# Fewer semaphore signals in three edge passes: counting steps in pairs, and the logit and state chains woven together

## The chip, the cores and the metric

One core of one Trainium2 chip runs the whole program. The metric is device time in microseconds of that core, as the median over runs.

## The reference

The reference is a graph network of 6250 nodes with 96 features and 200,000 edges sorted by destination, run as four blocks, each with a residual and a layer norm. What the change touches is the per-edge work of the first two blocks:

```python
# block 0, attention (4 heads): e = leaky_relu(a_src[src] + a_dst[dst], 0.2)
m = segment_max(e, dst); e = exp(e - m[dst]); denom = segment_sum(e, dst)
out = segment_sum((e / denom[dst])[:, :, None] * h[src], dst)
# block 1, twice: msg = x[src] @ W_msg + edge_attr @ W_edge
agg = segment_max(msg, dst)                   # 0 where a node has no edge
# blocks 2 and 3: sums over the edges of a node, five times (mean, mean, GCN x3)
```

## The kernel before, in words

The edges lie in order over 128 partitions, 1568 edges to a partition. An edge pass works through them in 196 slots (`SLOTS`) of 8 edges a partition (`S`). There are three such passes: the attention pass, and two maximum passes (`MAX_PASSES`). The five sums of the later blocks are matrix products with a table of edge counts, which is built in the two maximum passes; that stage has no part in the change.

**A slot of any pass.** POOL issues 8 indirect DMAs (L460, `gather_slot`), each fetching one table row for each partition into a ring of four slots (`RING`, tile CG). DVE turns the rows into running segment states with a scan, ACT copies the scanned states back into the ring slot (`rows_back`) and issues the store to `hist` (L928 or L974). POOL may refill a ring slot only when the store of the slot four earlier has landed (`hist_stored[r]`). So POOL is paced by its own issuing, or by the chain gather, DVE, ACT, store.

**Attention pass, DVE (L1456 to L1509).** `logits(u)`: sum of the two logit halves (L1465), leaky relu (L1466), running maximum by scan (L1469), decay terms (L1472), exponents (L1474, signals `exp_in`), maxima into the ring slot (L1476), carry (L1478). `states(u)`: rows times weights (L1486), carry (L1491), state scan (L1494, signals `scanned`). `link` signals `dve_step` and waits at once for that signal; `step` signals and waits later. The order is `logits(u + 1)`, `states(u)`. ACT (L912 to L956) does two exponentials (L938, L939), the resets of a later slot (L919), the broadcast of the scales (L943) and the copy back (L923), each with a signal of its own. Beside slots 4 to 36 DVE also does one `table_piece` a slot.

**Maximum passes, DVE (L1511 to L1573).** Each slot has 4 counting steps (`CS`). For step n DVE makes two one-hot tiles (L1529, L1532; the second signals `onehot_ready`), PE multiplies them with the low one-hots that ACT made (L713, L714; L714 signals `counted`) into one of three PSUM areas (psA, psB, psX, in turn), and DVE adds the product of step n - 2 to the running counts (L1537, signals `acc_ready`), which SP flushes to HBM (L574). Before its second one-hot, step n waits for `counted` of step n - 2: two steps may be on their way in PE. After the 4 steps DVE adds edge terms to the gathered rows (L1556) and scans twice (L1563, signals `scanned`). PE makes the edge terms of the slot first (L704, signals `eterm_ready`). ACT copies the resets (L965, signals `resets_ready`), copies back (L969), and makes the low one-hots: 8 squares (L989, signal `low_far`), waited for at once, then a relu (L993, signal `low_ready`). SP loads edge features two slots ahead (L583), behind the four flushes of the slot.

**Signals in a slot before**, counted in the code: attention 10 of DVE and 5 of ACT; maximum passes 11 of DVE, 5 of PE and 4 of ACT. The DMAs' own landings come on top and are as many before as after.

Of the kernel before, what the change touches and what calls it, by code (L numbers as in the profile page):

```python
# [17 lines left out]
S = 8  # L18
# [21 lines left out]
HALF = STEPS // 2  # L40
CW = GN * NB
# [60 lines left out]
def build(nc, x, src, dst, dst_before, src_tiles, dst_tiles, edge_attr, att_W, att_src, att_dst, gat_bias, proj_WT, proj_b, ln_g, ln_b,  # L102
# [58 lines left out]
    FAR = BUF[:, ring2 + 2 * CS * P:ring2 + 3 * CS * P].bitcast(BF16).rearrange("p (j a c) -> p j a c", j=CS, a=2)  # L161
# [161 lines left out]
    low_far = sem("low_far")  # L323
# [42 lines left out]
    scales_made = sem("scales_made")  # L366
# [4 lines left out]
    eterm_ready = [sem("eterm_ready0"), sem("eterm_ready1")]  # L371
# [155 lines left out]
    def _(sp):  # L527
# [21 lines left out]
        def edge_pass(q):  # L549
            if q in MAX_PASSES:  # L550
# [5 lines left out]
                for s in range(2):  # L556
                    if q == MAX_PASSES[1]:
                        sp.wait_ge(eterm_ready[s], ITERS)
                    sp.dma_start(EA[:, s, :, :], ea[:, 2 * s:2 * s + 2, :]).then_inc(ea_loaded[s], 16)
# [92 lines left out]
    def _(pe):  # L652
# [43 lines left out]
        def edge_terms(q):  # L696
# [3 lines left out]
            for u in range(SLOTS):  # L700
                s = u % 2
                pe.wait_ge(ea_loaded[s], 16 * (m * ITERS + u // 2 + 1))
                for a in range(2):
                    mm = pe.matmul(ETERM[:, s, a, 0:4 * DIM], EA[:, s, a, :], WE[:, m, :, :].rearrange("k c d -> k (c d)"),  # L704
                                   start=True, stop=True)
                mm.then_inc(eterm_ready[s], 1)
                for j in range(CS):
                    k = m * HALF + u * CS + j
                    sums = step_sums[k % 3]
# [5 lines left out]
            pe.wait_ge(acc_ready, (m + 1) * HALF + 2)  # L715
# [172 lines left out]
    def _(act):  # L888
# [25 lines left out]
        def attention_pass():  # L914
# [3 lines left out]
            def head_resets(u):  # L918
                nc.scalar.copy(reset_heads[:, u % 2, :, 1:K9],  # L919
                               reset[:, u * S:(u + 1) * S].unsqueeze(1).broadcast_to([P, HEADS, S])).then_inc(resets_ready, 1)  # L920
# [12 lines left out]
            head_resets(1)  # L933
            for u in range(SLOTS):
# [3 lines left out]
                nc.scalar.activation(EX[:, u % 2, 0, :, :], EX[:, u % 2, 0, :, :], ACT.Exp).then_inc(scales_made, 1)  # L938
# [947 lines left out]
```

## Time and profile before

| | us |
|---|---|
| runs before | 9809.52, 9786.81, 9767.25; median 9786.81 |
| profiled execution, first to last instruction | 9705.1 |
| busy: PE, DVE, ACT, POOL | 4073.0, 5048.9, 2904.4, 4813.6 |

No time of its own is given for the profiled execution beyond its span, so its span stands for it; the median of the runs is 81.7 us (0.8%) above. Core 0 runs alone. A busy time is work of an engine; idle time is listed with the line that it ends at and what was seen to release it. "remote" is a release for which the trace has no work of this core right before it, and "issue" is idle time for which the trace shows nothing. Times in a timeline count from the first instruction. The three passes lie at 108 to 2412, 2668 to 5191 and 5338 to 7862 us, measured from the first to the last gather.

### The profile page before, as it was taken

The numbers are of one execution on the slowest core, as the hardware profiler recorded it, in microseconds if no ns is written. First come the engines' busy times: TensorE is split into PE (matmuls) and PEld (weight loads), VectorE is DVE, ScalarE is ACT, GpSimd is POOL, SyncE is SP. The second block draws the span as 40 slices with busy tenths as digits, with TensorE's granted clock in tenths as the row PEclk, the third lists the DMA queues.
The fourth block names the chain that finished last, engine by engine and source line by source line (L and its number), as shares of the span: only waits on it lengthen the run. The fifth ranks groups of instructions, "written<-read, shape, count | busy, mean of one in ns | idle before, by whom it ended". The sixth has DMA issues, their size and how long they took to land.

```text
span 9705.1 us, 71574 instructions
## 1 busy us (share of the span) xinstructions
PE 4073.0 (42%) x19184; PEld 2488.5 (26%) x19184; DVE 5048.9 (52%) x10097; ACT 2904.4 (30%) x5669; POOL 4813.6 (50%) x5030
## 2 busy tenths in 40 slices
PE   1100000000444444344443344444444438999999
PEld 1000000000311111111112111111111118999999
DVE  4554444444456656565564565666565647522222
ACT  0222222222244444444442344444444420000000
POOL 6566667666166556555654665555555640000000
PEclk6555555555555555555555555555555559999999
DMA  4222222222133333333332333333333325567667
GB/s 124 70 82 77 75 74 80 74 77 73 28 104 109 103 99 111 96 103 99 103 103 70 101 107 97 103 105 101 103 101 100 106 73 202 212 235 262 226 236 251
DMA packets 642173, 1129.74 MB, mean 116 GB/s; under 512 B 164844, under 2 KB 422271, under 8 KB 641618
## 3 DMA queue, kind: packets, MB, share of 16 engines
q1 hardware_dynamic: 360112, 437.17, 14.5%
q0 software_dynamic: 159184, 251.10, 12.4%
q10 hardware_dynamic: 122578, 438.40, 11.4%
q14 instruction: 223, 1.83, 0.1%
q8 instruction: 76, 1.25, 0.1%
HBM read 713.46 MB, written 412.70 MB: 116 GB/s over the span
## 4 chain that ended last, share of the span: by engine, by line
DVE 41%; another core or an unknown queue 23%; PE 17%; issue 9%; POOL 7%; DMA 2%; ACT 1%; DVEq 0%; SPq 0%; POOLq 0%; ACTq 0%
DVE BUF L1537 9%; POOL CG L460 6%; PE psX L734 5%; PE psB L734 5%; PE psA L734 5%; DVE BUF L1532 4%; DVE XTQ L1563 4%; DVE STG L1563 4%; DVE BUF L1529 4%; DVE XTQ L1556 3%; DVE STG L1556 3%; DVE EX L1474 1%; PE psO L677 1%; DVE terms L1472 1%
## 5 line engine op out<-in xcount | busy, mean ns | idle before, releaser
L460 POOL DMA_INDIRECT CG<-table,BUF x4704 | 4484.3, 953 | 3031.4 <-DMA hist<-CG 1408.9
L1532 DVE TENSOR_SCALAR BUF<-iota,EG 128x392 bf16<-128x392 f16 x1568 | 528.9, 337 | 1880.0 <-remote 1617.1
L704 PE MATMUL psO<-WE,BUF 128*128 128x384 f32 x1568 | 1104.6, 858 | 313.2 <-DMA BUF<-in_edge_attr 197.3
L989 ACT ACTIVATE BUF<-iota,EG 128x128 bf16<-128x128 f16 x3136 | 958.1, 387 | 348.9 <-remote 139.4
L965 ACT COPY psX<-BUF 128x384 f32<-128x384 f32 x392 | 189.0, 482 | 2536.9 <-DVE XTQ L1563 1461.9
L777 PE MATMUL psA<-ident,F 128*100 128x128 f32 x1 | 0.5, 452 | 1893.9 <-DVEq L1439 1893.9
L486 POOL CAST CG<-EG x35 | 27.8, 794 | 1359.8 <-DVEq L1205 1359.8
L704 PEld LDWEIGHTS psO<-WE,BUF 128*128 128x128 f32 x1568 | 467.4, 320 | 736.2 <-issue 416.2
L713 PE MATMUL psB<-BUF 128*128 128x392 bf16 x523 | 240.7, 460 | 872.3 <-issue 616.6
L713 PE MATMUL psA<-BUF 128*128 128x392 bf16 x523 | 241.1, 461 | 851.5 <-issue 577.2
L713 PE MATMUL psX<-BUF 128*128 128x392 bf16 x522 | 241.0, 462 | 845.0 <-issue 592.4
L1529 DVE TENSOR_SCALAR BUF<-iota,EG 128x392 bf16<-128x392 f16 x1568 | 514.7, 328 | 102.5 <-DVE BUF L1537 31.3
L938 ACT ACTIVATE EX<-EX 128x36 f32<-128x36 f32 x196 | 45.6, 233 | 1691.3 <-issue 587.3
L734 PE MATMUL psB<-CG,BUF 128*128 128x288 bf16 x4018 | 509.2, 287 | 7.1 <-DMA BUF<-counts 6.7
L734 PE MATMUL psA<-CG,BUF 128*128 128x288 bf16 x4018 | 509.2, 287 | 6.5 <-DMA BUF<-counts 6.2
L734 PE MATMUL psX<-CG,BUF 128*128 128x288 bf16 x3969 | 501.1, 287 | 0.6 <-POOL CG L489 0.6
L734 PEld LDWEIGHTS psB<-CG,BUF 128*128 128x128 bf16 x4018 | 494.9, 142 | 10.0 <-issue 7.2
L734 PEld LDWEIGHTS psA<-CG,BUF 128*128 128x128 bf16 x4018 | 494.9, 142 | 9.2 <-POOL CG L489 7.1
L734 PEld LDWEIGHTS psX<-CG,BUF 128*128 128x128 bf16 x3969 | 488.4, 142 | 1.8 <-POOL CG L489 0.8
L777 PEld LDWEIGHTS psA<-ident,F 128*100 128x100 f32 x1 | 0.2, 158 | 1894.2 <-DVEq L1439 1894.2
L993 ACT ACTIVATE BUF<-BUF,ones 128x1024 bf16<-128x1024 bf16 x392 | 450.0, 1148 | 13.0 <-ACT BUF L989 0.3
L1563 DVE TENSOR_TENSOR_SCAN XTQ<-psX,XTQ 128x432 f32<-128x432 f32 x392 | 392.7, 1043 | 6.7
(284 smaller groups left out, 7560.8 us busy)
## 6 DMA issues: line engine op xcount, KB each, us to landing
BUF<-counts SPq DMA_DIRECT2D x245, 784.0 KB
BUF<-counts ACTq DMA_DIRECT2D x245, 784.0 KB
counts<-BUF SPq DMA_DIRECT2D x1572, 98.0 KB
hist<-CG ACTq DMA_DIRECT2D x392, 384.0 KB
hist<-CG ACTq DMA_DIRECT2D x196, 416.0 KB
CG<-table,BUF POOLq DMA_INDIRECT x4704
BUF<-in_edge_attr SPq DMA_DIRECT2D x392, 128.0 KB
table<-TB SPq DMA_DIRECT2D x14, 336.0 KB
```

The costliest lines, as they stand in the source:

```text
L460: pool.indirect_dma_start(out=rows_in[:, u % RING, k, :], out_offset=None, in_=tab, in_offset=bass.IndirectOffsetOnAxis(ap=SRC[:, u * S + ...
L704: mm = pe.matmul(ETERM[:, s, a, 0:4 * DIM], EA[:, s, a, :], WE[:, m, :, :].rearrange("k c d -> k (c d)"), start=True, stop=True)
L713: pe.matmul(sums, LOW[:, s, j, 0, :], RHS[:, j, 0, :], start=True, stop=False)
L734: mm = pe.matmul(sums[:, 0:3 * DIM], CNT16[:, B % 3, b:b + NB * (P - 1) + 1:NB], PARTS[:, b, :], start=b == 0, stop=b == NB - 1, skip_grou ...
L965: nc.scalar.copy(reset_cols[:, :, 1:K9], reset[:, u * S:(u + 1) * S].unsqueeze(1).broadcast_to([P, DIM // 2, S])).then_inc(resets_ready, 1)
L989: far = nc.scalar.activation(FAR[:, j, a, :], iota16[:, 0:P], ACT.Square, bias=STEP[:, 2 + a, u * CS + j:u * CS + j + 1], scale=-1.0)
L993: nc.scalar.activation(LOW[:, u % 2, :, :, :], FAR, ACT.Relu, bias=ones[:, 0:1], scale=-1.0).then_inc(low_ready, 1)
L1529: ts(RHS[:, j, 0, :], iota16[:, :], STEP[:, 0, n:n + 1], None, ALU.is_equal)
L1532: ts(RHS[:, j, 1, :], iota16[:, :], STEP[:, 1, n:n + 1], None, ALU.is_equal).then_inc(onehot_ready, 1)
L1537: stt(ACC[:, j, :], ACC[:, (j - 1) % CS, :], STEP[:, 4, n:n + 1], step_sums[k % 3], ALU.mult, ALU.add).then_inc(acc_ready, 1)
L1556: tt(max_cols[b][:, :, 1:K9].rearrange("p c (a k) -> p c a k", a=2), ROWSW[:, r, :, :].rearrange("p (a k) c -> p c a k", a=2), ETERM[:, s, ...
L1563: scan = nc.vector.tensor_tensor_scan(out=columns, data0=reset_flat, data1=columns, initial=0.0, op0=ALU.add, op1=ALU.max)
```

## The change

It removes, merges and moves signals and waits; every sum, scan, product and DMA stays. In the maximum passes:

- DVE's counting steps go in pairs. A pair gives one `onehot_ready` and one `acc_ready`, PE one `counted`; pair p waits for `counted` of pair p - 1, the pair issued just before.
- PE no longer signals the edge terms: they come before the pairs in PE's order, so `counted` covers them. SP's loads of edge features wait for the first pair of the slot instead, and SP's flushes go two at a time.
- ACT makes the squares one slot ahead, in two buffers (`FAR`), so that the relu need not wait for squares just made; the relu gives no signal (the squares after it do), and neither do the resets (`block_done` does).

In the attention pass the chains are woven so that another instruction stands between a producer and its consumer and an older signal covers both. Signals in a slot after: attention 5 of DVE and 3 of ACT; maximum passes 6 of DVE, 2 of PE and 2 of ACT.

```diff
@@ PE, edge_terms
-                mm.then_inc(eterm_ready[s], 1)
-                for j in range(CS):
-                    k = m * HALF + u * CS + j
-                    if j == 0:
-                        pe.wait_ge(low_ready, m * SLOTS + u + 1)
-                    pe.wait_ge(onehot_ready, k + 1)
-                    pe.matmul(sums, LOW[:, s, j, 0, :], RHS[:, j, 0, :], start=True, stop=False)
-                    pe.matmul(sums, LOW[:, s, j, 1, :], RHS[:, j, 1, :], start=False, stop=True).then_inc(counted, 1)
+                pe.wait_ge(low_ready, m * (SLOTS + 1) + u + 2)
+                for h in range(2):
+                    pe.wait_ge(onehot_ready, m * PAIRS + 2 * u + h + 1)
+                    for j in (2 * h, 2 * h + 1):
...
+                    mm.then_inc(counted, 1)
@@ SP, edge_pass
-                    sp.wait_ge(acc_ready, m * HALF + u * CS + j + 3)
+                    if j % 2 == 0:
+                        sp.wait_ge(acc_ready, m * PAIRS + 2 * u + j // 2 + 1)
...
-                    sp.wait_ge(eterm_ready[s], u // 2 + m * ITERS + 1)
+                    sp.wait_ge(counted, m * PAIRS + 2 * u + 1)
@@ ACT, running_pass
+            low_squares(0)
             low_one_hots(0)
+            low_squares(1)
...
-                if u + 1 < SLOTS:
+                if u + 2 < SLOTS:
                     low_one_hots(u + 1)
+                    low_squares(u + 2)
@@ ACT, attention_pass
-                nc.scalar.activation(EX[:, u % 2, 0, :, :], EX[:, u % 2, 0, :, :], ACT.Exp).then_inc(scales_made, 1)
+                nc.scalar.activation(EX[:, u % 2, 0, :, :], EX[:, u % 2, 0, :, :], ACT.Exp)
...
-                act.wait_ge(scales_made, u + 1)
+                act.wait_ge(exp_done, u + 1)
@@ DVE, running_pass
+            def pair(p):
+                n, done = 2 * p, m * PAIRS + p
+                if p and done > 1:
+                    dve.wait_ge(acc_ready, done - 1)
+                one_hot(n, 0)
+                one_hot(n, 1)
+                if p:
+                    flushed_before(n - 2)
+                one_hot(n + 1, 0)
+                if p:
+                    dve.wait_ge(counted, done)
+                    accumulate(n - 2)
+                    flushed_before(n - 1)
+                one_hot(n + 1, 1).then_inc(onehot_ready, 1)
+                if p:
+                    dve.wait_ge(onehot_ready, done + 1)
+                    accumulate(n - 1).then_inc(acc_ready, 1)
...
+                pair(2 * u)
...
+                nc.vector.tensor_copy(max_cols[b][:, :, 0:1], max_cols[1 - b][:, :, S:K9])
+                pair(2 * u + 1)
...
-                dve.wait_ge(dve_step, steps[0])
-                dve.wait_ge(resets_ready, q * SLOTS + u + 1)
-                dve.wait_ge(eterm_ready[s], m * ITERS + i + 1)
...
+                if u:
+                    dve.wait_ge(block_done[(u - 1) % RING], q * LAPS + (u - 1) // RING + 1)
@@ DVE, attention_pass
+            def exponents(u):
+                tt(scale_terms, maxima[:, 0:HEADS * K9], resets_of(u), ALU.add)
+                step(nc.vector.tensor_copy(ROWS0[:, u % RING, :, SW:W0], max9[:, :, 1:K9].rearrange("p h k -> p k h")))
+                dve.wait_ge(dve_step, steps[0])
+                tt(EX[:, u % 2, :, :, :].rearrange("p a h k -> p a (h k)"), terms[:, :, :, :].rearrange("p a h k -> p a (h k)"),
+                   maxima[:, 1:].unsqueeze(1).broadcast_to([P, 2, HEADS * K9]), ALU.subtract).then_inc(exp_in, 1)
...
+            def slot(u):
+                after = u + 1 < SLOTS
+                if after:
+                    carry_maxima(u)
+                    logits(u + 1)
+                carry_state(u)
+                if after:
+                    dve.wait_ge(dve_step, steps[0])
+                    leaky()
+                product(u)
+                dve.wait_ge(dve_step, steps[0])
+                if after:
+                    running_maxima(u + 1)
+                states(u)
+                if after:
+                    dve.wait_ge(scanned, u + 1)
+                    exponents(u + 1)
```

## Rows read from the trace of the kernel before

**Rows 1.** The page's first line: span of the profiled execution.
```profile
span 9705.1 us, 71574 instructions
```
**Rows 2.** Stretches from first to last gather, attention and first maximum pass.
```profile
core 0: us, PE busy (x) PEld busy (x) DVE busy (x) ACT busy (x) POOL busy (x), PEclk, DMA share, GB/s
108.00:2412.00 2304.00, 54.51 (x260) 26.86 (x260) 1081.62 (x2098) 531.75 (x974) 1544.14 (x1618) 0.51 0.29 77
2668.00:5191.00 2523.00, 1099.01 (x2329) 342.05 (x2330) 1533.78 (x3102) 1083.71 (x2142) 1494.80 (x1568) 0.57 0.36 103
```
**Rows 3.** POOL's waits for stores, by pass; the second is attention from 560 us on.
```profile
POOL CG L460 <- DMA hist<-CG: 282.4, 68, 20.6
...
POOL CG L460 <- DMA hist<-CG: 205.5, 62, 5.5
...
POOL CG L460 <- DMA hist<-CG: 565.9, 52, 14.7
...
POOL CG L460 <- DMA hist<-CG: 560.6, 51, 16.4
```
**Rows 4.** Timeline of POOL, first maximum pass: start, us, what, idle before.
```profile
3978.33 0.94 POOL L460 DMA_INDIRECT CG<-table,BUF  x1 [13.45 <-DMA hist<-CG]
3979.58 0.94 POOL L460 DMA_INDIRECT CG<-table,BUF  x1 [0.30 <-issue]
```
**Rows 5.** Timeline of DVE, one fast slot of the first maximum pass.
```profile
3973.38 0.30 DVE L1529 TENSOR_SCALAR BUF<-iota,EG 128x392 bf16<-128x392 f16 x1
...
3979.25 2.00 DVE L1563 TENSOR_TENSOR_SCAN STG<-psX,STG 128x432 f32<-128x432 f32 x2
3981.17 0.30 DVE L1529 TENSOR_SCALAR BUF<-iota,EG 128x392 bf16<-128x392 f16 x1
```
**Rows 6.** Timeline of DVE, the slow slot before it.
```profile
3932.83 0.46 DVE L1529 TENSOR_SCALAR BUF<-iota,EG 128x392 bf16<-128x392 f16 x1
3940.74 0.32 DVE L1532 TENSOR_SCALAR BUF<-iota,EG 128x392 bf16<-128x392 f16 x1 [7.45 <-issue]
...
3946.32 0.32 DVE L1532 TENSOR_SCALAR BUF<-iota,EG 128x392 bf16<-128x392 f16 x1 [4.30 <-remote]
...
3956.84 0.32 DVE L1532 TENSOR_SCALAR BUF<-iota,EG 128x392 bf16<-128x392 f16 x1 [3.67 <-remote]
...
3968.07 0.32 DVE L1532 TENSOR_SCALAR BUF<-iota,EG 128x392 bf16<-128x392 f16 x1 [10.02 <-remote]
```
**Rows 7.** Timeline of PE in the same slow slot.
```profile
3931.62 0.53 PE L714 MATMUL psX<-BUF 128*128 128x392 bf16 x1
3932.32 0.51 PE L713 MATMUL psA<-BUF 128*128 128x392 bf16 x1 [0.17 <-DVE BUF L1532]
3932.62 0.53 PE L714 MATMUL psA<-BUF 128*128 128x392 bf16 x1
```
**Rows 8.** Groups by form, first maximum pass: busy and mean ns, idle before.
```profile
L1532 DVE TENSOR_SCALAR BUF<-iota,EG 128x392 bf16<-128x392 f16 x776 | 262.2, 338 | 929.3 <-remote 810.3 <-issue 109.4 <-PE psA L714 6.6
...
L1537 DVE SCALAR_TENSOR_TENSOR BUF<-BUF,EG,psX 128x392 bf16<-128x392 bf16 x258 | 158.0, 613 | 0.0
```
**Rows 9.** The same groups of ACT: squares and copy back.
```profile
L989 ACT ACTIVATE BUF<-iota,EG 128x128 bf16<-128x128 f16 x1560 | 476.6, 387 | 169.0 <-issue 68.2 <-remote 62.3 <-PE psA L714 13.3
...
L969 ACT COPY CG<-STG 128x768 f32<-128x768 f32 x97 | 152.0, 1567 | 0.0
```
**Rows 10.** Timeline of DVE, one slow slot of the attention pass.
```profile
1860.86 2.03 DVE L1494 TENSOR_TENSOR_SCAN XTQ<-psX,XTQ 128x900 f32<-128x900 f32 x1 [3.03 <-remote]
...
1867.10 0.20 DVE L1472 TENSOR_TENSOR terms<-maxima,reset_heads 128x36 f32<-128x36 f32 x1 [1.80 <-remote]
1868.50 0.23 DVE L1474 TENSOR_TENSOR EX<-terms,maxima 128x72 f32<-128x72 f32 x1 [1.21 <-DVE terms L1472]
...
1869.90 0.17 DVE L1478 COPY terms<-maxima 128x4 f32<-128x4 f32 x1 [1.07 <-DVE EX L1474]
...
1874.86 2.03 DVE L1494 TENSOR_TENSOR_SCAN STG<-psX,STG 128x900 f32<-128x900 f32 x1 [3.03 <-remote]
```
**Rows 11.** Timeline of POOL in that slot.
```profile
1868.31 0.94 POOL L460 DMA_INDIRECT CG<-table,BUF  x1 [4.33 <-DMA hist<-CG]
```

More of the change, by code:

```diff
@@ L40 @@
 HALF = STEPS // 2
+PAIRS = HALF // 2
 CW = GN * NB
@@ L557, in edge_pass @@
                     if q == MAX_PASSES[1]:
-                        sp.wait_ge(eterm_ready[s], ITERS)
+                        sp.wait_ge(counted, PAIRS)
                     sp.dma_start(EA[:, s, :, :], ea[:, 2 * s:2 * s + 2, :]).then_inc(ea_loaded[s], 16)
@@ L918, in head_resets @@
             def head_resets(u):
-                nc.scalar.copy(reset_heads[:, u % 2, :, 1:K9],
-                               reset[:, u * S:(u + 1) * S].unsqueeze(1).broadcast_to([P, HEADS, S])).then_inc(resets_ready, 1)
+                return nc.scalar.copy(reset_heads[:, u % 2, :, 1:K9],
+                                      reset[:, u * S:(u + 1) * S].unsqueeze(1).broadcast_to([P, HEADS, S]))
             def rows_back(u):
@@ L964, in column_resets @@
             def column_resets(u):
-                nc.scalar.copy(reset_cols[:, :, 1:K9],
-                               reset[:, u * S:(u + 1) * S].unsqueeze(1).broadcast_to([P, DIM // 2, S])).then_inc(resets_ready, 1)
+                return nc.scalar.copy(reset_cols[:, :, 1:K9],
+                                      reset[:, u * S:(u + 1) * S].unsqueeze(1).broadcast_to([P, DIM // 2, S]))
             def rows_back(u):
@@ L1193, in _ @@
         dve.sem_inc(sums_ready, 3)
-        dve.sem_inc(counted, 1)
-        dve.sem_inc(acc_ready, 2)
         dve.sem_inc(again_used, 1)
@@ L1482, in states, with carry_state, product @@
+            def carry_state(u):
+                b = u % 2
+                if u:
+                    dve.wait_ge(scanned, u)
+                step(nc.vector.tensor_copy(state_cols[b][:, :, 0:1], state_cols[1 - b][:, :, S:K9]))
+            def product(u):
                 r, b = u % RING, u % 2
@@ L1499, in attention_pass @@
             dve.sem_inc(pass_begun, 1)
-            logits(0)
+            link(logits(0))
+            link(leaky())
+            dve.wait_ge(resets_ready, 1)
+            link(running_maxima(0))
+            exponents(0)
             for u in range(SLOTS):
-                if u + 1 < SLOTS:
-                    logits(u + 1)
-                states(u)
+                slot(u)
                 piece = u - PIECES_FROM
@@ L1539, in running_pass @@
             for u in range(SLOTS):
-                i, s = u // 2, u % 2
                 r, b = u % RING, u % 2
-                for j in range(CS):
-                    one_hots(u * CS + j)
-                    if u * CS + j >= 2:
-                        accumulate(u * CS + j - 2)
-                    if j == 0:
-                        if u:
-                            dve.wait_ge(scanned, q * SLOTS + u)
-                        step(nc.vector.tensor_copy(max_cols[b][:, :, 0:1], max_cols[1 - b][:, :, S:K9]))
+                pair(2 * u)
@@ L1565, in running_pass @@
                 scan.then_inc(scanned, 1)
-            for n in range(HALF - 2, HALF):
-                dve.wait_ge(acc_ready, m * HALF + n + 2)
-                dve.wait_ge(counted, m * HALF + n + 2)
-                accumulate(n)
+            dve.wait_ge(counted, (m + 1) * PAIRS)
+            dve.wait_ge(acc_ready, (m + 1) * PAIRS - 1)
+            flushed_before(HALF - 2)
+            link(accumulate(HALF - 2))
+            flushed_before(HALF - 1)
+            accumulate(HALF - 1).then_inc(acc_ready, 1)
             dve.wait_ge(scanned, (q + 1) * SLOTS)
             dve.wait_ge(block_done[RING - 1], (q + 1) * LAPS)
-            dve.wait_ge(counted, (m + 1) * HALF + 1)
             dve.sem_inc(end_free, 1)
```

104 lines of the change are left out of this document (53 added, 51 removed).

## The prediction

> **What bounds the kernel now.** I read the stretches of the three passes first, then POOL's waits in them, then the timelines. The attention pass takes 2304 us and the first maximum pass 2523 [rows 2]; together the three take some 7350 of the span of 9705.1 [rows 1]. No engine fills them: in the maximum pass POOL is busy 1495 us, DVE 1534, PE 1099. But a gather takes 0.94 us and the next starts 0.30 later [rows 4], 1.25 in all, so 196 slots of 8 gathers need 196 x 9.98 = 1956 us of POOL in each pass. What a pass takes beyond that is POOL waiting for a store: 282.4 us in attention, 565.9 and 560.6 in the maximum passes [rows 3]. That wait is what a change on DVE, PE or ACT can win, and 1956 is the floor.
>
> Why do stores come late? Not for want of DVE: a fast slot runs from one L1529 at 3973.38 to the next at 3981.17, 7.8 us [rows 5], less than POOL's 9.98. Some slots are slow. In the one before it DVE sits idle ahead of L1532, which waits for `counted` of step n - 2, again and again: 7.45, 4.30, 3.67, 10.02 us [rows 6]. Over the pass that is 929.3 us [rows 8]. PE is not the one that is late: its product into psX ends at 3931.62 + 0.53 = 3932.15, the one into psA at 3933.15 [rows 7], yet the L1532 that waits for the first goes at 3940.74 and the one that waits for the second at 3946.32 [rows 6]. Products that ended 1.0 us apart are noticed 5.6 us apart, 8.6 and 13.2 us late. So what is late is the signal, and it stands in a line: between 3940.74 and 3968.07 five signals of PE pass (four `counted` and the slot's `eterm_ready`), one each 27.33 / 5 = 5.5 us. A fast slot shows nothing of it. The line ends after POOL pauses: the wait before 3978.33 is 13.45 us, so its last gather ended at 3964.88 [rows 4], and the last long wait of DVE at 3968.07 [rows 6]. I read this as signals being let through slowly while gathers are issued and many signals are wanted. What the limit is made of, the rows don't say.
>
> In attention the same shows on DVE's own signals: L1472, L1474 and L1478 go at 1867.10, 1868.50 and 1869.90, exactly 1.40 apart, with 1.80, 1.21 and 1.07 us idle, and the state scan waits 3.03; the slot takes 1874.86 - 1860.86 = 14.0 us [rows 10], and POOL waits 4.33 in it [rows 11].
>
> **The change, maximum passes.** PE's signals fall from 5 to 2 a slot. At one each 5.5 us a slow slot needs 2 x 5.5 = 10.9 us where it needed 27.3. That is 0.9 over POOL's 9.98, so POOL hardly gets ahead, and where it does, it pauses and DVE does 7.8 us slots. Bounds of the slot: 9.98 below (POOL), 10.9 above. I take 10.5, in the middle, since the line of signals empties at each pause. A pass is then 196 x 10.5 = 2058 instead of 2523: -465, twice -930.
>
> What the change adds there, edit by edit:
> - Pair p waits for the pair issued just before it, where a step waited for the last but one. After the last one-hot of a pair PE needs four products. L713 to L714 start 0.30 apart and the last lasts 0.53 [rows 7], so about 1.5 us. DVE has one accumulation of 0.61 and three one-hots of 0.34 [rows 8] to do meanwhile, which overlap a little: 1.3 to 1.6. Exposed: nothing to 0.2 us in the middle of a slot, nothing at its start, where the sum and the scans (over 3.4 us) lie between. That makes at most 8.0 us of a 7.8 us slot, hidden under POOL's 9.98. With that cover gone it would cost 196 x 0.2 = 39 us a pass.
> - The wait of DVE for its own `onehot_ready` before the second accumulation: nothing up to 1.4 us a pair, by rows 10, the nearest for DVE's own signals. At 1.4 a slot is 7.8 + 0.2 + 2.8 = 10.8, inside the bound above. Nothing taken: in rows 6 PE and SP pick up DVE's signals, and no L1537 waits at all [rows 8].
> - SP's flushes leave in twos, the first up to a step later. An L1537 waits for the flush of four steps before; it shows 0.0 us idle [rows 8] with the flush a slot old, and it stays a slot old. The load of edge features now waits for `counted`, but stands behind the flushes of its slot as before, so it moves by no more than a pair (2.3 us). It is needed by the next but one slot's L704. Free while a slot is 10 us.
> - ACT: the scans now wait for the copy back of the slot before (L969, 1.57 us [rows 9], after a reset copy). From 3973.38 to 3979.25 DVE needs 5.9 us before its scans [rows 5], so it is covered by over 3 us. One set of eight squares more stands ahead of a pass: at most 8 x 0.387 = 3.1 us [rows 9], twice, against POOL's first four slots (40 us): nothing.
> - Signals of DVE (11 to 6) and ACT (4 to 2) that go: below nothing, no cost. In a fast slot they cost nothing and I count no gain.
>
> **The change, attention.** DVE's own signals fall from 10 to 5. At 1.40 us each, five fewer make the 14.0 us slot 7.0. At the other end, each of the five that stay costs the largest wait shown between small operations, 1.80, on top of 5.0 us of work (14.0 less the idle time in that slot): 14.0. By the order of the new chain I get 8.4: scan 2.0, then `dve_step`, `exp_in`, `carry_state` and `exp_done` one behind the other at 1.4 with the small operations in their shadow, and the product 1.7 hiding the last; it is below 9.98, so POOL sets the slot. What goes is the waiting from 560 us on, 205.5 us [rows 3]; the 77 before lie in the start and beside table pieces with long chains of links, which stay. -205.
>
> **The sum.** -930 - 205 = -1135. The profiled execution would have a span of 9705 - 1135 = 8570. The median of the runs, 9786.8, is 82 us above that span; kept, it gives 8652, and I say 8650. With the slots at 9.98: 9786.8 - 566 - 561 - 205 = 8455. At 10.9: a pass of 2136, so -387 twice and -205: 8808.
>
> **The rivals.**
> - *A lone signal is as late as one in a line.* The rows show PE's signals with others ahead of them; whether a single one is prompt during gathers they don't. If it takes 5.5 us after its product, a pair is a loop of 5.5 and some 1.9 of work, and a slow slot is 14.8 us. Slow and fast slots then mix as in attention, where slots of 14.0 give a pass of 2304 / 196 = 11.75 us a slot. Maximum passes of 2304 each: -219 twice, -205: about 9145 (9000 to 9300).
> - *The line is held by landings, not by these signals.* Gathers and flushes bring as many landings as before. For: the waits end soon after POOL pauses. Against: the even 5.5 us between PE's signals. Then only attention gains: 9787 - 205 = 9580.
> - *Signals cost nothing.* Then PE was held by something that the profile lacks, and the change is worth what a fast slot shows for it, 0: 9787. For: in the fast slot each L1529 starts right behind. Against: the even spacing in rows 6 and 10. The Trainium skill speaks for this one (VectorE: DVE Perf Modes, the section on the DRAIN): eight copies with a semaphore each took as long as with one after the last. It says so of DVE alone with no gathers beside it, and rows 10 disagree with it, 1.40 us a signal; by that rule attention would keep its 2304 us.
> - *Slower: the pair exposes PE's delay in every slot.* Its place is the wait for `counted` of the pair before. A step had two of its kind under way, a pair has none. If a lone signal takes 5.5 us in all slots and no fast ones come between, a pass is 196 x 14.8 = 2901, 378 longer: +756 - 205, about 10,340. It decides from a delay of 4.8 us in each pair on: 2 x (4.8 + 1.9) = 13.4 against 12.9 now. Against it: the fast slot of rows 5, 7.8 us with five signals of PE in it while POOL gathers again from 3978.33.
>
> That the change fails to remove the signals is excluded by its text.
>
> **How the numbers follow.** My case has 0.55, the lone signal 0.26, landings alone 0.06, no cost 0.07, slower 0.06. The time is that of the first, 8650; its own range is 8450 to 8810. With the second the range is 8430 to 9300, which leaves out 0.19. A measurement of this kernel can tell about 0.5% from no change (its runs lie within 0.43%). Faster by more: 0.55 + 0.26 + 0.06 = 0.87; within: 0.07; slower: 0.06.
>
> **What would show it.** Right: the 52 and 51 waits of POOL in the maximum passes go or shrink to under 100 us together, first to last gather 1960 to 2140 us, slots near 10 with no L1532 or its like idle for 4 us or more, and attention near 2100 with POOL's waits left only before 560 us. The lone signal: waits of some 5 us before nearly every first accumulation of a pair while gathers run. Landings: slow slots of 20 us and more remain. Wrong altogether: POOL's waits stay above 500 us a pass.

## The result, and the profile after

The changed kernel takes 10,010.6 us (median of 4 runs, 10,006.3 to 10,019.0) beside 9798.2 for the kernel before (4 runs, 9767.3 to 9840.2): a ratio of 1.0199, interval 1.0168 to 1.0231. It is 2% slower, where 8650 us was forecast. Its profiled execution has a span of 10,010.0 us, 304.9 above the one before [rows 1]; the medians of the runs lie 212.4 us apart, since the traced execution of the kernel before was shorter than each of its timed runs. What follows explains the traces' difference.

The page of the changed kernel, first its span and the chain that ended last, then the groups of the accumulations (busy, mean ns, idle before):

```profile
span 10010.0 us, 71174 instructions
...
DVE 37%; another core or an unknown queue 27%; PE 17%; issue 10%; POOL 6%; ACT 2%; DMA 1%; DVEq 0%; SPq 0%; ACTq 0%; POOLq 0%
...
L1579 DVE SCALAR_TENSOR_TENSOR BUF<-BUF,EG,psA 128x392 bf16<-128x392 bf16 x523 | 324.2, 620 | 769.8 <-remote 662.9
L1579 DVE SCALAR_TENSOR_TENSOR BUF<-BUF,EG,psX 128x392 bf16<-128x392 bf16 x522 | 323.6, 620 | 739.3 <-remote 667.3
L1579 DVE SCALAR_TENSOR_TENSOR BUF<-BUF,EG,psB 128x392 bf16<-128x392 bf16 x523 | 324.2, 620 | 727.4 <-remote 662.7
```

The wait for TensorE's `counted` stood ahead of L1532 before; it now stands ahead of the first accumulation of a pair, L1579. Its three groups are idle 769.8 + 739.3 + 727.4 = 2236.5 us over both maximum passes. In the kernel before, this row of its page is the counterpart:

```profile
L1532 DVE TENSOR_SCALAR BUF<-iota,EG 128x392 bf16<-128x392 f16 x1568 | 528.9, 337 | 1880.0 <-remote 1617.1
```

So the wait that the change was expected to shrink grew by 356 us. The stretches of the three passes (attention and the two maximum passes) and POOL's waits for stores in them, all of the changed kernel, the second wait again attention from 560 us on:

```profile
107.00:2414.00 2307.00, 50.92 (x260) 25.54 (x260) 1056.93 (x2098) 530.78 (x973) 1544.55 (x1618) 0.51 0.29 77
2669.00:5344.00 2675.00, 1017.35 (x2330) 393.50 (x2331) 1531.95 (x3101) 1063.46 (x2150) 1481.99 (x1568) 0.58 0.34 97
5492.00:8172.00 2680.00, 1037.90 (x2332) 399.92 (x2332) 1529.68 (x3102) 1063.50 (x2150) 1481.50 (x1568) 0.57 0.34 97
```
```profile
POOL CG L460 <- DMA hist<-CG: 289.0, 81, 19.4
...
POOL CG L460 <- DMA hist<-CG: 216.0, 75, 5.2
...
POOL CG L460 <- DMA hist<-CG: 727.2, 49, 16.9
...
POOL CG L460 <- DMA hist<-CG: 732.2, 48, 16.6
```

Attention is unchanged: 2307 us against 2304 [rows 2], waits of 289.0 against 282.4 [rows 3]. The first maximum pass is 152 us longer (2675 against 2523), and POOL's waits in the two grew from 565.9 + 560.6 [rows 3] to 727.2 + 732.2, by 333 us. The whole loss lies in the maximum passes.

One slow slot of the first maximum pass, on DVE, PE and POOL (the first DVE row is of the slot ahead of it):

```profile
4072.45 0.62 DVE L1579 SCALAR_TENSOR_TENSOR BUF<-BUF,EG,psX 128x392 bf16<-128x392 bf16 x1 [2.22 <-issue]
...
4083.66 0.62 DVE L1579 SCALAR_TENSOR_TENSOR BUF<-BUF,EG,psB 128x392 bf16<-128x392 bf16 x1 [5.26 <-remote]
...
4101.16 0.62 DVE L1579 SCALAR_TENSOR_TENSOR BUF<-BUF,EG,psA 128x392 bf16<-128x392 bf16 x1 [14.82 <-remote]
```
```profile
4084.78 0.49 PE L712 MATMUL psA<-BUF 128*128 128x392 bf16 x1 [7.28 <-issue]
...
4085.71 0.53 PE L713 MATMUL psB<-BUF 128*128 128x392 bf16 x1
```
```profile
4094.95 0.94 POOL L460 DMA_INDIRECT CG<-table,BUF  x1 [0.30 <-issue]
4111.03 0.94 POOL L460 DMA_INDIRECT CG<-table,BUF  x1 [15.13 <-DMA hist<-CG]
```

PE's pair ends at 4085.71 + 0.53 = 4086.24; DVE goes on at 4101.16, 14.9 us later, and 5.3 us after POOL's last gather has ended (4095.89). POOL starts again only at 4111.03. The same holds for the pauses of POOL of 5 us or more in the two maximum passes (94 before, 98 after; medians 13.2 and 15.3 us). The last idle time of DVE over 0.6 us that ends in such a pause ends 4.3 us after POOL stopped in the kernel before (median of 86; a tenth under 2.1) and 5.4 us in the changed one (96; a tenth under 4.7).

Slow slots come every fourth slot, mostly, in both kernels. Mean times of the slow slot and of the three ahead of it, from the nearest to the farthest, are 27.0, 8.0, 8.2 and 7.9 us before, and 28.5, 10.5, 8.3 and 8.0 now (101 and 96 slow slots). So the slow slot is as long as ever, with two signals of TensorE in it where there were five, and more than half of the loss lies in the slot just ahead of it: there DVE waited 0.07 us for `counted` before and waits 2.50 us now.

In attention a slow slot of the changed kernel still takes 1863.09 - 1849.06 = 14.0 us, as before [rows 10], with five signals of DVE in place of ten:

```profile
1849.06 2.00 DVE L1521 TENSOR_TENSOR_SCAN XTQ<-psX,XTQ 128x900 f32<-128x900 f32 x1
...
1853.11 0.23 DVE L1492 TENSOR_TENSOR EX<-terms,maxima 128x72 f32<-128x72 f32 x1 [1.72 <-remote]
1854.51 0.20 DVE L1498 COPY terms<-maxima 128x4 f32<-128x4 f32 x1 [1.17 <-DVE EX L1492]
...
1860.12 0.19 DVE L1481 SCALAR_TENSOR_TENSOR terms<-terms 128x32 f32<-128x32 f32 x1 [5.18 <-remote]
...
1863.09 2.00 DVE L1521 TENSOR_TENSOR_SCAN STG<-psX,STG 128x900 f32<-128x900 f32 x1
```

One step of 1.40 is still there, between two operations of which the second waits (1853.11 to 1854.51). From L1498 at 1854.51 to L1481 at 1860.12 stand L1498, L1478 and L1505, of which only the last signals. They start within 0.2 us of each other, and yet L1481, which waits for that signal, comes 5.61 us later, four times 1.40 for three operations. Over the whole slot the count fits: ten operations of DVE in both kernels, and 10 x 1.40 = 14.0.

In the maximum passes two counts can be told apart, since signals and instructions of PE stand in different proportions. Two releases of DVE that follow each other in the kernel before, both after a long wait, with what PE did between the two products waited for:

```profile
4002.27 0.32 DVE L1532 TENSOR_SCALAR BUF<-iota,EG 128x392 bf16<-128x392 f16 x1 [3.42 <-remote]
...
4018.37 0.32 DVE L1532 TENSOR_SCALAR BUF<-iota,EG 128x392 bf16<-128x392 f16 x1 [14.37 <-issue]
```
```profile
3995.67 2.93 PE L704 MATMUL psO<-WE,BUF 128*128 128x384 f32 x4 [1.57 <-DMA BUF<-in_edge_attr]
3998.39 0.53 PE L713 MATMUL psB<-BUF 128*128 128x392 bf16 x1
3998.72 0.45 PE L714 MATMUL psB<-BUF 128*128 128x392 bf16 x1
```

They are 16.10 us apart. I took all such neighbours, both idle for over 1 us before, of which the second goes while gathers are issued:

| between two releases | signals of PE | instructions of PE | us (median) | number | us for each signal | us for each instruction |
|---|---|---|---|---|---|---|
| before, no edge terms | 1 | 4 | 5.60 | 42 | 5.6 | 1.40 |
| before, edge terms | 2 | 12 | 16.10 | 47 | 8.1 | 1.34 |
| after, no edge terms | 1 | 8 | 10.62 | 80 | 10.6 | 1.33 |

An instruction is a matmul or its weight load; the two come in equal numbers, so a price by the matmul fits as well. In the third row half of the 80 lie near 10.5 and the others near 11.2, as the two rows of DVE above do (4083.66 - 4072.45 = 11.21). Counted by signals the price differs by almost two; counted by instructions it is 1.33 to 1.40 in all three. So in these traces the late time goes by PE's instructions, and a signal for two steps comes about twice as far apart as a signal for one.

### The profile page after: what moved, and what is told of

Read it like the earlier page. It is cut to its first block, busy times and chain, and to the rows that moved or that the text cites. A ratio compares the mean times of both kernels' runs of the same rounds, so it can differ in the third digit from the quotient of the medians.

```text
span 10010.0 us, 71174 instructions
## 1 busy us (share of the span) xinstructions
PE 3927.0 (39%) x19184; PEld 2592.6 (26%) x19184; DVE 5024.3 (50%) x10096; ACT 2859.0 (29%) x5669; POOL 4784.9 (48%) x5030
## 4 chain that ended last, share of the span: by engine, by line
DVE 37%; another core or an unknown queue 27%; PE 17%; issue 10%; POOL 6%; ACT 2%; DMA 1%; DVEq 0%; SPq 0%; ACTq 0%; POOLq 0%
DVE BUF L1574 7%; DVE BUF L1579 7%; POOL CG L460 5%; PE psX L734 5%; PE psB L734 5%; PE psA L734 5%; DVE XTQ L1624 4%; DVE STG L1624 4%; DVE XTQ L1613 3%; DVE STG L1613 3%; DVE STG L1513 1%; DVE XTQ L1513 1%; DVE XTQ L1521 1%; DVE STG L1521 1%
## 5 line engine op out<-in xcount | busy, mean ns | idle before, releaser
L460 POOL DMA_INDIRECT CG<-table,BUF x4704 | 4455.2, 947 | 3369.7 <-DMA hist<-CG 1748.5
L705 PE MATMUL psO<-WE,BUF 128*128 128x384 f32 x1568 | 1069.4, 835 | 154.0 <-DMA BUF<-in_edge_attr 91.3
L1574 DVE TENSOR_SCALAR BUF<-iota,EG 128x392 bf16<-128x392 f16 x3136 | 898.2, 328 | 18.6 <-DMA EG<-step_rows 18.6
L1579 DVE SCALAR_TENSOR_TENSOR BUF<-BUF,EG,psA 128x392 bf16<-128x392 bf16 x523 | 324.2, 620 | 769.8 <-remote 662.9
L1579 DVE SCALAR_TENSOR_TENSOR BUF<-BUF,EG,psX 128x392 bf16<-128x392 bf16 x522 | 323.6, 620 | 739.3 <-remote 667.3
L1579 DVE SCALAR_TENSOR_TENSOR BUF<-BUF,EG,psB 128x392 bf16<-128x392 bf16 x523 | 324.2, 620 | 727.4 <-remote 662.7
```

What stands on the lines that cost most here:

```text
L460: pool.indirect_dma_start(out=rows_in[:, u % RING, k, :], out_offset=None, in_=tab, in_offset=bass.IndirectOffsetOnAxis(ap=SRC[:, u * S + ...
L1574: return ts(RHS[:, n % CS, a, :], iota16[:, :], STEP[:, a, n:n + 1], None, ALU.is_equal)
L1579: return stt(ACC[:, j, :], ACC[:, (j - 1) % CS, :], STEP[:, 4, n:n + 1], step_sums[(m * HALF + n) % 3], ALU.mult, ALU.add)
```

## The experiments

**First four: one part alone, more signals, fewer and more instructions.**

woven_only is the kernel before with the attention pass of the changed one, on DVE and ACT. after_signals is the changed kernel with a signal added to instructions without one, on semaphores that nobody reads:

```diff
-                pe.matmul(sums, LOW[:, s, j, 0, :], RHS[:, j, 0, :], start=True, stop=False)
+                pe.matmul(sums, LOW[:, s, j, 0, :], RHS[:, j, 0, :], start=True, stop=False).then_inc(spare_pe, 1)
...
-                    leaky()
+                    leaky().then_inc(spare, 1)
```

no_terms leaves out TensorE's edge terms from slot 2 of each maximum pass on (eight of the 24 instructions of a slot); two_more adds two tiny memsets of DVE to each slot of attention:

```diff
-                for a in range(2):
+                for a in range(2 if u < 2 else 0):
```
```diff
                     logits(u + 1)
+                nc.vector.memset(Q[:, 0:1], 0.0)
...
                 product(u)
+                nc.vector.memset(most_all[:, :], 0.0)
```

> The attention pass of the changed kernel with the maximum passes of the kernel before. Theory I (a slow slot is paid by the instruction: in the slow state an engine gives up about 1.4 us for each instruction that it has done before its next signal is let through, however many of them signal): the attention pass is as before (2304 us, slow slots of 14.0 us, since DVE still has 10 instructions a slot), the maximum passes 2523 each, the time that of before within 0.5%. Theory S (paid by the signal): attention gains 100 us or more. If the loss of 2% came from the attention part, this kernel shows it (about 9950 to 10,010); if it came from the pairs, it doesn't.

> The changed kernel, with a signal that nobody waits for on the 5 DVE instructions a slot of attention that have none, and in the maximum passes on 10 of PE's 12 matrix instructions a slot and on 5 more of DVE's: more signals than even the kernel before. Theory I: nothing changes, 10,010 within 0.5%, slow slots 14.0 and 27.3 us. Theory S: a slow slot of the maximum passes grows from 27 to 60 us and more (12 signals of PE at 5.5), the time to over 12,000.

> The changed kernel without PE's edge terms from the third slot of a maximum pass on (the sum then takes stale terms; the 8 edge-term instructions of PE a slot, weight loads included, go, 24 to 16). They carry no signal. Theory I: slow slots shrink from 27.3 to about 27.3 x 16/24 = 18.2 us, four slots from 55 to about 46, a maximum pass from 2675 to about 2250, the time to about 9150. Theory S: no signal goes, so no change but the 2 to 3 us of PE work a slot that lie beside other work: 10,010. A third theory, that PE's signals are held until POOL stops whatever PE does: slow slots stay at 27 us and the time at 10,010 too.

> The changed kernel with two more DVE instructions a slot of attention, sets of one column without a signal, about 0.06 us of work each. Theory I: slow slots of attention 12 x 1.4 = 16.8 us instead of 14.0, the pass longer by 100 to 400 us, the time 10,110 to 10,400. Theory S: 10,010 and slow slots of 14.0.

Measured beside them, the kernel before itself took 8144.9 us (19 runs, 8139.6 to 8153.3), not 9798. woven_only took 8147.1 (ratio 1.0000, 0.9991 to 1.0010), after_signals 8130.0 (0.9981, 0.9971 to 0.9991), no_terms 8121.0 and two_more 8122.9 in one run each. None of the four shows a slow slot (the longest slot of a maximum pass is under 13 us), so none of the numbers expected for one could be tested. In this condition the signals added, the instructions taken out and those added all cost nothing that shows. That says nothing yet of the condition of the first runs.

**Next three: both kernels again, each with its trace, and the pairs alone.** after_again and before_again are the two kernels unedited; pairs_only is the changed kernel with the old attention pass on ACT and DVE.

> The changed kernel, unedited. Two theories. W: the wait for signals of TensorE and VectorE while gathers are issued belongs to the condition in which the two kernels were first timed (9798 and 10,011 us); where the kernel before takes about 8145 us it is absent, GpSimd's gathers bound both, and the changed kernel comes within 0.5% of it, about 8130 us (ratio 0.996 to 1.000), with maximum pass slots of 10 us and no slots of 27. I: the loss is in the code itself (an exposed wait of VectorE for the pair just before), then the changed kernel is longer than the kernel before in either condition, by about 300 us (8450, ratio 1.037). Where the kernel before takes about 9800 us beside it, both expect 10,010 us.

> The kernel before, unedited, for its own trace beside the others. W, if it takes about 8145 us: first to last gather of a maximum pass 1970 us in place of 2522, GpSimd idle under 60 us a pass in place of 565, every slot about 10 us with no fourth slot of 29, and the signal of TensorE's step at VectorE within 1 us of the end of the matmul. I: the same slow slots as in the first trace, at any total.

> The changed kernel with the attention pass of the kernel before, on ScalarE and VectorE: one part of the change alone. W: with GpSimd as the bound of both passes, the same as the kernel before within 0.5%, 8130 to 8150 us; where the kernel before takes about 9800 us beside it, 10,010 us, since the attention pass gave nothing and the maximum passes all of the loss. I: 300 us above the kernel before in either.

On this second chip the kernel before took 8163.5 us (14 runs, 8158.2 to 8170.1), the changed kernel 8141.1 (7 runs, 8138.8 to 8143.5; ratio 0.9971, 0.9960 to 0.9983), pairs_only 8137.6 (0.9970, 0.9959 to 0.9981). before_again's page, and its first maximum pass:

```profile
span 8165.2 us, 71574 instructions
...
POOL 57%; PE 20%; issue 19%; DVE 3%; ACT 1%; DMA 1%; DVEq 0%; POOLq 0%; SPq 0%; ACTq 0%
...
L1532 DVE TENSOR_SCALAR BUF<-iota,EG 128x392 bf16<-128x392 f16 x1568 | 556.9, 355 | 6.2 <-PE psB L714 3.2
```
```profile
2340.00:4321.00 1981.00, 1179.43 (x2350) 332.53 (x2350) 1565.95 (x3130) 1091.27 (x2155) 1502.87 (x1568) 0.56 0.44 132
```

The instructions are the same 71,574. The idle time ahead of L1532 is 6.2 us in place of 1880.0, the pass 1981 us in place of 2523, and the chain that ended last is POOL's. Matched instruction by instruction, the two traces of this one kernel drift apart by 1540 us, 1458 of them between the first gather and the last; from some 200 us behind the last gather they keep step within 1.6 us to the end. In attention, the operations that stood 1.40 us apart [rows 10] now follow at 0.23 and 0.29:

```profile
1101.24 0.20 DVE L1472 TENSOR_TENSOR terms<-maxima,reset_heads 128x36 f32<-128x36 f32 x1
1101.47 0.26 DVE L1474 TENSOR_TENSOR EX<-terms,maxima 128x72 f32<-128x72 f32 x1
1101.76 0.17 DVE L1478 COPY terms<-maxima 128x4 f32<-128x4 f32 x1
```

The records of signals differ too. The trace of the first condition has 40,352 semaphore updates, before_again 144,116 for the same program. In the two maximum passes 20,855 are left where there are 95,452, and behind the last gather 11,493 where there are 12,005. So in the first traces "remote" and "issue" often mean that the record of the signal is missing. Of the updates of `counted`, 571 of 1028 stand within 0.1 us of the recorded end of a product in the first trace, and 1568 of 1569 in before_again.

So there are two conditions for the same kernel. In the one of the first runs the signals of PE and DVE come late while gathers are issued; in this one (the prompt condition, below) they don't, and POOL's 1568 gathers set a maximum pass. Whether what lost the records also made the engines late, or the recording itself did, no run tells; the timed runs of the first condition (9767 to 9840 us) are no shorter than the traced execution. Of the last three expectations W stands, and their I (the loss is in the code in either condition) falls. The changed kernel's accumulations hardly wait either, here in after_again:

```profile
L1579 DVE SCALAR_TENSOR_TENSOR BUF<-BUF,EG,psB 128x392 bf16<-128x392 bf16 x523 | 323.1, 618 | 19.3 <-PE psX L713 5.5
L1579 DVE SCALAR_TENSOR_TENSOR BUF<-BUF,EG,psA 128x392 bf16<-128x392 bf16 x523 | 323.1, 618 | 21.0 <-PE psB L713 5.8
L1579 DVE SCALAR_TENSOR_TENSOR BUF<-BUF,EG,psX 128x392 bf16<-128x392 bf16 x522 | 322.4, 618 | 15.2
```

In the prompt condition the change is worth 0.3%, from the pairs alone: the maximum pass of the changed kernel is 1966 us against 1981, POOL's L460 busy 1487.91 against 1502.87 in it. Its gathers are 10 ns shorter each, and why was not tested:

```profile
2343.00:4309.00 1966.00, 1106.14 (x2348) 393.08 (x2348) 1577.15 (x3130) 1069.08 (x2155) 1487.91 (x1568) 0.57 0.45 133
```

**A late TensorE made on purpose.** The condition of the first runs did not come up on any of the four chips that ran the experiments (8144.9, 8163.5, 8144.3 and 8163.3 us for the kernel before). The runs of this part and the next are one for each kernel. What could be tested is the changed kernel's answer to a late signal. In every fourth slot the first counting matmul is issued 64 times more, in both kernels, with the same result:

```diff
+                        for _ in range(64 if j == 0 and u % 4 == 3 else 0):
+                            pe.matmul(sums, LOW[:, s, j, 0, :], RHS[:, j, 0, :], start=True, stop=True)
                         pe.matmul(sums, LOW[:, s, j, 0, :], RHS[:, j, 0, :], start=True, stop=False)
```

after_lag_steps gives the changed kernel a signal of TensorE for each step again, and DVE a wait for each; after_steps is that without the 64:

```diff
-                    dve.wait_ge(counted, done)
+                    dve.wait_ge(counted, 2 * done - 1)
                     accumulate(n - 2)
...
                     dve.wait_ge(onehot_ready, done + 1)
+                    dve.wait_ge(counted, 2 * done)
                     accumulate(n - 1).then_inc(acc_ready, 1)
```

> The kernel before with TensorE late on purpose: in every fourth slot of a maximum pass the first counting matmul of the slot is issued 64 times more, each with the same result, ahead of the real one (0.33 us apart at 1.2 GHz, so 21 us; 10.5 us at 2.4 GHz). It stands in for the late signal of TensorE in the first traces, where the kernel before takes 8163 us. At 21 us four slots take VectorE 31 us of work and about 20 of stall, 51 in place of 40: 49 x 11 x 2 = 1080 us more, 9240 us; at the full clock about 8200. Both theories expect the same here; it is the base for the next two.

> The changed kernel with the same 64 matmuls in every fourth slot. Theory E (exposure): the pair of steps gives VectorE less other work to do while TensorE is late, and it needs four matmuls for its one signal where the step needed two, so each late signal stalls VectorE 2 to 3 us longer than in before_lag: 98 x 2 to 3 = 200 to 300 us above before_lag, of which the first traces' loss of 306 us is an instance. Theory N: the order of waits gives away nothing, a late TensorE costs both the same, and the two are within 60 us of each other; then the loss in the first traces came from something in the state of the chip that lags with the instructions themselves.

> As after_lag, but TensorE signals each step again (four signals a slot), and VectorE waits for the first step of a pair before it adds that step, and for the second before it adds the second. E by grain (VectorE waits for matmuls of the second step that it does not need yet): most of the excess of after_lag over before_lag goes, 100 to 250 us less than after_lag. E by place (the add stands two one-hots earlier than before, whatever the number of signals): within 60 us of after_lag. N: all three alike.

> after_lag_steps without the late matmuls: the changed kernel with one signal of TensorE for each step and the finer waits. Where the kernel before takes about 8150 us, GpSimd is the bound and all theories expect the changed kernel's time within 15 us, 8141. Where the kernel before takes about 9800 us: if each signal has its price, above the changed kernel's 10,010 us by 100 us or more; if the loss is the grain of the wait, 9700 to 9850 us.

Measured, with 8144.3 for the kernel before beside them: before_lag 8358.8, after_lag 8461.5, after_lag_steps 8415.4, after_steps 8128.2. The extra matmuls ran mostly at the 2.4 GHz level, some 11 us a burst, so before_lag is nearer the 8200 of its expectation than the 9240. (The 8163 us that this expectation gives to the first traces is a time of the other condition.) after_lag stands 102.7 above before_lag: E has its sign and a third to a half of its size, N (within 60) falls. The grain of the wait gives back 46 of it, which by the stated bounds (within 60) is E by place. One late slot of each, DVE and PE, of before_lag:

```profile
3016.21 0.32 DVE L1534 TENSOR_SCALAR BUF<-iota,EG 128x392 bf16<-128x392 f16 x1 [9.82 <-PE psA L716]
```
```profile
3004.49 11.35 PE L714 MATMUL psA<-BUF 128*128 128x392 bf16 x64 [0.62 <-DVE BUF L1534]
3015.68 0.33 PE L715 MATMUL psA<-BUF 128*128 128x392 bf16 x1
```

and of after_lag:

```profile
3039.80 0.62 DVE L1581 SCALAR_TENSOR_TENSOR BUF<-BUF,EG,psA 128x392 bf16<-128x392 bf16 x1 [10.10 <-PE psB L715]
```
```profile
3028.32 10.77 PE L713 MATMUL psA<-BUF 128*128 128x392 bf16 x64 [2.19 <-DVE BUF L1576]
3038.93 0.33 PE L714 MATMUL psA<-BUF 128*128 128x392 bf16 x1
```

Before, DVE falls idle at 3016.21 - 9.82 = 3006.39, 1.90 us after the burst began: it had other work for so long. It is released 0.53 us after the real products begin (3015.68). In the changed kernel it falls idle at 3029.70, 1.38 us after the burst began, and is released 0.87 us after they begin (3038.93). So it has 0.52 us less to do beside a late TensorE and waits for 0.34 us more of products: 0.86 us for each late signal in this pair of slots.

**Three late slots of four.** As above, with 24, 40 and 64 extra matmuls in slots 1, 2 and 3 of each four:

```diff
-                        for _ in range(64 if j == 0 and u % 4 == 3 else 0):
+                        for _ in range((0, 24, 40, 64)[u % 4] if j == 0 else 0):
```

> The kernel before with TensorE late in three slots of four: 24, 40 and 64 extra matmuls ahead of the first counting matmul of the slot (4, 6.6 and 10.6 us at 2.4 GHz), near the pattern of the first traces (stalls of 3, 1 and 14 us in four slots there). From before_lag: 10.2 us of stall for 64 matmuls and 32.0 us of other time in four slots; here 20 and 32, so 52 in place of 40.4: 98 x 11.7 = 1150 us above 8144, 9290 us. It is the base for the next two.

> The changed kernel with the same three late slots of four. One late signal in four slots cost it 1.06 us more of stall than the kernel before (102.7 us in 98 cycles); the first traces show 3.1 us more in four slots. If the excess is paid once for each late signal, three of them cost 3 x 1.06 x 98 = 310 us: 9600 us, about the loss of the first runs (306). If it is paid once in the cycle whatever the number of late signals, 100 us: 9390, and two thirds of the first loss have another cause.

> As after_lags, with a signal of TensorE for each step and a wait for each step in VectorE. In after_lag_steps this took back 46 of 103 us. Paid once for each late signal: it takes back 3 x 46 = 140 us, 9460 us. Paid once in the cycle: 9345 us.

before_lags took 9236.3 us (9290 expected), after_lags 9866.5, 630 more, after_lags_steps 9618.7. The excess is twice the larger of the two that were forecast, and the finer signals take back 248 of it where 140 was forecast. One windows row of each (600 us of the first maximum pass: PE, PE's weight loads, DVE, ACT, POOL, PEclk, DMA share, GB/s), before_lags and then after_lags, shows a part of why:

```profile
2600.00:3200.00 600.00, 447.65 (x2052) 218.58 (x2050) 371.40 (x754) 262.35 (x517) 358.36 (x375) 0.90 0.37 104
```
```profile
2600.00:3200.00 600.00, 430.37 (x1821) 212.62 (x1822) 323.22 (x665) 227.42 (x457) 311.27 (x330) 0.82 0.32 92
```

The changed kernel was granted a lower clock, 0.82 against 0.90, and its late slots got later. One burst of 64 took 10.77 us in before_lags and 13.39 in after_lags:

```profile
3000.30 10.77 PE L714 MATMUL psA<-BUF 128*128 128x392 bf16 x64 [2.70 <-DVE BUF L1534]
```
```profile
3023.34 13.39 PE L713 MATMUL psX<-BUF 128*128 128x392 bf16 x64 [3.75 <-DVE BUF L1576]
```

In the mean of the 98 bursts of 64 it is 10.8 and 13.2 us, at a granted clock of 1.00 and 0.81 within them; bursts of 40 took 8.5 us in both. The wait ahead of each burst is longer too, 3.6 us in place of 2.7 ahead of those of 64: a pair of one-hots is handed over as one, so PE stands still longer before it starts. That the longer standing still lowered the clock fits these rows and was not tested by itself. Taken from the start of its first extra matmul to the end of its last and summed over the 294 late slots, the bursts are 2335.5 us before and 2698.8 after, 363 of the 630. What is left is the waiting that the bursts don't explain. The rows that wait, of before_lag and after_lag in turn, over both passes:

```profile
L1534 DVE TENSOR_SCALAR BUF<-iota,EG 128x392 bf16<-128x392 f16 x1568 | 509.9, 325 | 1024.9 <-PE psA L716 346.9
```
```profile
L1581 DVE SCALAR_TENSOR_TENSOR BUF<-BUF,EG,psB 128x392 bf16<-128x392 bf16 x523 | 323.5, 619 | 382.8 <-PE psX L715 369.7
L1581 DVE SCALAR_TENSOR_TENSOR BUF<-BUF,EG,psA 128x392 bf16<-128x392 bf16 x523 | 323.5, 618 | 374.9 <-PE psB L715 360.7
L1581 DVE SCALAR_TENSOR_TENSOR BUF<-BUF,EG,psX 128x392 bf16<-128x392 bf16 x522 | 323.0, 619 | 356.6 <-PE psA L715 342.9
```

| kernel | late slots | bursts, us | DVE's wait, us | hidden in each late slot, us |
|---|---|---|---|---|
| before_lag | 98 | 1139.6 | 1024.9 | 1.17 |
| after_lag | 98 | 1135.4 | 1114.3 | 0.22 |
| after_lag_steps | 98 | 1133.0 | 1061.8 | 0.73 |
| before_lags | 294 | 2335.5 | 1887.1 | 1.53 |
| after_lags | 294 | 2698.8 | 2538.1 | 0.55 |
| after_lags_steps | 294 | 2541.5 | 2282.8 | 0.88 |

The last column is bursts less wait, by late slot. The pairs lose 0.95 us of cover for a late signal in the first set and 0.98 in the second, so the price is paid for each late signal, and about a half and a third of it is the grain of the wait.

## Why the prediction was wrong

- **What bounds the kernel.** Right for its trace: the stores came late, DVE stood ahead of L1532 for a signal, and the recorded products of PE had ended long before. POOL's 1956 us as the floor of a pass held too; in the prompt condition a pass takes 1966 to 1981.
- **The step that failed: "one each 27.33 / 5 = 5.5 us", and with it "a slow slot needs 2 x 5.5 = 10.9 us where it needed 27.3".** Five signals in 27.33 us was a count of what had passed in the slot, and I took it for a price. With two signals a slow slot still takes 28.5 us in the mean, so each would cost 14. What the traces show in its place is a price by PE's instruction, 1.33 to 1.40 us, with 5.6, 8.1 and 10.6 us for a signal as there are 4, 6 or 8 instructions to it; both kernels have 24 a slot. The trace at hand could have told. In the slot of rows 6 the spacing looked "even" (5.58 us for one signal up to 3946.32, 11.23 for two up to 3968.07) only because POOL stopped at 3964.88: the update of `eterm_ready` is recorded at 3965.93, 9.1 us behind the `counted` before it, and the next `counted` 2.1 us behind that. While gathers go on, two signals with the edge terms between them take 16.10 us, not 10.9. The whole -930 hung on it.
- **Attention, -205, failed in the same way.** "At 1.40 us each, five fewer make the 14.0 us slot 7.0": it stayed 14.0, with ten operations of DVE in it before and after. Here the number of operations was not varied in the condition that matters, so that they set the 14.0 is a reading. Measured: +3 us for the pass.
- **The exposed pair wait, "nothing to 0.2 us in the middle of a slot".** In the prompt condition that holds: L1579 idles 19.3 + 21.0 + 15.2 = 55.5 us in 784 pairs, 0.07 us each, and POOL covers it. Its mistake was to price the wait for a prompt TensorE only. When TensorE is late, the cover is gone, and what counts is how much less work DVE has beside it than before: 0.95 to 0.98 us for each late signal. The wait in the first traces grew by 2236.5 - 1880.0 = 356 us, 3.6 us in each of 98 cycles of four slots. DVE has 2.9 waits over 0.6 us in such a cycle (289 before, 283 after, in 98 cycles), so 2.9 x 0.95 to 0.98 = 2.8. The size is right within a quarter, and the new wait of 2.50 us in the slot ahead of the slow one, where DVE had work enough before, fits the same loss of cover. In that condition itself it was not tried, so the cause of the first loss is in part argued.
- **The rivals.** The slower one named the right place, the wait for the pair just before, and the reason ("a pair has none" under way), but wanted a lone signal of 5.5 us in every slot and gave 10,340. It needed neither: two of the three fast slots stayed near 8 us, and the loss came in the slow slot and the one ahead of it. "Signals cost nothing" was right on signals: in the first runs halving them took nothing off a slow slot, and in the prompt condition adding them back cost nothing (8130.0 against 8144.9, 0.9981 of the kernel before, where the changed kernel without them was 0.9971 on another chip). The Trainium skill (VectorE: DVE Perf Modes, the section on the DRAIN) had it that copies of DVE with a semaphore each take no longer than with one after the last; by that rule attention would keep its 2304 us, and the trace agrees with 2307. I set it aside for rows 10, where 1.40 us stood between operations that also signalled, and took that time for the signals'. The rival on landings predicted that slow slots of 20 us and more remain in the maximum passes, and they did, but attention did not gain.
- **What is open.** Why the signals of PE and DVE come late during gathers in one condition and not in the other was not found, nor whether it belongs to the chip, the time or the recording. In the changed kernel's first trace it ends some 5 us after POOL stops gathering, and in both it goes with the number of PE's instructions rather than signals; both are read from traces, and the four kernels that vary the numbers ran where the condition was absent.

after_steps, the version that the late runs favour among the pairs, took 8128.2 us in its one run beside 8144.3: the gain of the pairs in the prompt condition, within what one run can tell. Where TensorE was made late, the kernel before is still the better one (8358.8 against 8415.4, 9236.3 against 9618.7).

## What to carry to other kernels

A quotient such as "27 us for five signals" is no price until a second count in the same stretch (instructions, bytes, slots) has been ruled out; look for two stretches in which the counts differ. When handshakes are merged, write down what the waiting engine has to do between the signal that it gives and the one that it needs, before and after, and price the difference at the latest partner that the trace shows, not at the usual one. A kernel whose trace shows idle time that no engine explains should be timed again, on another chip too, before it is tuned against that idle time, and the records of signals in its trace should be counted.

## What was unexpected of the hardware

- One kernel with the same 71,574 instructions took 9767 to 9840 us in its first runs and 8139 to 8170 on four chips later, 17% less. In the two traces 95% of the difference (1458 of 1540 us) lies between the first and the last gather. The gathers themselves took the same, 4484.3 us busy then and 4501.0 later.
- In the first condition signals of PE came 1.33 to 1.40 us apart for each matmul and weight load between them, whether there were 4, 8 or 12 (5.60, 10.62 and 16.10 us), and a slow attention slot took 14.0 us for ten operations of DVE, five or ten of them signalling. In the other, operations 1.40 us apart in the first went at 0.23 and 0.29.
- The trace of that condition kept 40,352 records of semaphore updates where the same program left 144,116 in the other, and they are missing in the passes with gathers.
- The granted clock went along with the loss: with the same extra matmuls the kernel in which TensorE waits longer was granted 0.82 and the other 0.90, and a burst of 64 took 13.39 us in place of 10.77.
